# Graph attention over edges: values gathered by indirect DMA, and leaky ReLU split in two parts

## The reference, cut to what matters

```
Xq = H @ W_lin.T ; Xv = H @ W_val.T            # per node, split in 4 heads
e  = sum_d leaky_relu(Xq[src] + Xq[dst], 0.2) * a
e  = e + log(adj[src, dst] + 1e-8)
attn = softmax of e over the edges with the same src
Y[src] = sum over edges of attn * Xv[dst]
x  = layernorm(x + Y @ W_out.T)
```

## Time and profile before

| | us |
|---|---|
| median of 3 runs | 875.0 |
| all runs | 874.92, 875.27, 875.0 |
| span of the profiled execution | 876.8 |

### The profile page before, as it was taken

The page is one execution under the profiler, slowest core; times in us unless marked ns, Lnnn a source line. Parts: engine busy times, 40 slices in busy tenths (PEclk is TensorE's granted clock), DMA queues, the critical chain, the costliest instruction groups (busy, mean ns, idle before and its releaser), DMA issues.

```text
span 876.8 us, 15203 instructions
## 1 busy us (share of the span) xinstructions
PE 856.3 (98%) x5228; PEld 744.9 (85%) x5228; DVE 698.4 (80%) x1572; ACT 607.1 (69%) x1117; POOL 237.5 (27%) x562
## 2 busy tenths in 40 slices
PE   8999999999999999999999999999999999999996
PEld 7888888878778789999998887878887999999885
DVE  5888888868888878777777777767987787897986
ACT  3778878886766766767676666666896677776454
POOL 0233333340000000000000001003474355666766
PEclk9999999999999999999999999999999999999999
DMA  4222221000000001000000086777155010111223
GB/s 139 74 61 61 61 61 49 1 1 1 1 1 0 1 1 49 1 1 1 1 2 0 12 180 145 163 167 154 45 125 117 14 37 26 37 38 37 59 64 84
DMA packets 30988, 45.43 MB, mean 52 GB/s; under 512 B 2593, under 2 KB 23745, under 8 KB 27841
## 3 DMA queue, kind: packets, MB, share of 16 engines
q1 hardware_dynamic: 27680, 27.34, 10.8%
q0 software_dynamic: 2304, 16.78, 9.4%
q10 hardware_dynamic: 928, 0.35, 0.2%
HBM read 19.29 MB, written 8.39 MB: 32 GB/s over the span
## 4 chain that ended last, share of the span: by engine, by line
PE 79%; DVE 13%; ACT 4%; issue 2%; DMA 1%; POOL 1%; DVEq 0%; POOLq 0%; ACTq 0%
PE psum L505 7%; PE psum L506 7%; PE psum L507 7%; PE psum L523 6%; PE psum L519 6%; PE psum L520 6%; PE psum L1344 5%; PE psum L1266 5%; PE psum L412 3%; PE psum L454 3%; PE psum L1357 3%; PE psum L388 2%; PE psum L389 2%; PE psum L387 2%; PE psum L1324 2%
## 5 line engine op out<-in xcount | busy, mean ns | idle before, releaser
L646 ACT ACTIVATE work<-psum,bias 128x512 f32<-128x512 f32 (+1 forms) x408 | 232.1, 622 | 27.4 <-PE psum L523 26.0
L505 PE MATMUL psum<-hT_hi,w_hi 128*128 128x512 f32 (+1 forms) x406 | 148.2, 365 | 3.3 <-ACT work L646 2.8
L506 PE MATMUL psum<-hT_lo,w_hi 128*128 128x512 f32 (+1 forms) x406 | 146.5, 361 | 0.0
L507 PE MATMUL psum<-hT_hi,w_lo 128*128 128x512 f32 (+1 forms) x406 | 146.4, 361 | 0.0
L627 ACT ACTIVATE work<-work 128x512 f32<-128x512 f32 (+1 forms) x112 | 63.8, 570 | 108.9 <-DVE work L967 71.9
L978 DVE TENSOR_TENSOR work<-work 128x512 f32<-128x512 f32 (+1 forms) x111 | 68.6, 618 | 54.0 <-ACT work L627 54.0
L519 PE MATMUL psum<-hs_hi,w_hi 128*128 128x512 f32 (+1 forms) x288 | 103.9, 361 | 1.1 <-DVE hs_hi L912 0.9
L523 PE MATMUL psum<-hs_lo,w_hi 128*128 128x512 f32 (+1 forms) x288 | 104.5, 363 | 0.0
L520 PE MATMUL psum<-hs_hi,w_lo 128*128 128x512 f32 (+1 forms) x288 | 103.2, 358 | 0.0
L1172 POOL DMA_DIRECT2D hT_lo<-hT_hi x8 | 7.5, 937 | 351.3 <-DVE hT_lo L914 330.8
L505 PEld LDWEIGHTS psum<-hT_hi,w_hi 128*128 128x128 f32 x406 | 76.4, 188 | 17.4 <-ACT work L646 5.2
(11 more groups left out here) (225 smaller groups left out, 1902.9 us busy)
## 6 DMA issues: line engine op xcount, KB each, us to landing
work<-x_by_batch SPq DMA_DIRECT2D x32, 256.0 KB, 2.7
x_stage<-x_by_state SPq DMA_DIRECT2D x8, 1024.0 KB, 5.6
hT_lo<-hT_hi POOLq DMA_DIRECT2D x8, 1024.0 KB, 9.8
hT_lo<-x_stage POOLq DMA_DIRECT2D x8, 1024.0 KB, 7.2
out<-x_kept SPq DMA_DIRECT2D x31, 256.0 KB, 2.3
work<-L_gnn_Wih SPq DMA_DIRECT2D x4, 256.0 KB, 2.9
work<-L_gnn_Whh SPq DMA_DIRECT2D x3, 256.0 KB, 3.1
out<-x_kept SPq DMA_DIRECT2D x2, 128.0 KB, 2.3
```

The source lines that it names most:

```text
L505: pe.matmul(out, w_hi[:, w, g, :], xh, start=True, stop=False)
L506: pe.matmul(out, w_hi[:, w, g, :], xl, start=False, stop=False)
L507: mm = pe.matmul(out, w_lo[:, w, g, :], xh, start=False, stop=(t == 0))
L646: op = act.activation(gate[s][g][:, 0:ph.width], psum[:, 4 * s + g, 0:ph.width], ACT.Tanh if g == G else ACT.Sigmoid, bias=bias[:, b:b + 1])
```

## The change

The value product is no longer split. ACT copies it from the accumulator to the SBUF tensor `values`, SP stores it to a tensor in DRAM, and for every four tiles POOL issues two indirect DMAs (one for each half of the edges) that fetch for each edge the row of its `dst`. `value_gather` and `value_lo` are gone; `weight_values` multiplies in place.

Leaky ReLU becomes 0.8 relu(z) + 0.2 z. The linear part of the score is linear in the query, so the query weights get 4 more columns (0.2 W a, one for each head), and a query tile is 132 columns wide. Three batches fit in the accumulator bank, the fourth goes to another one. POOL copies the 4 columns of `xq_hi` and `xq_lo` to `linear` (`keep_linear`), where they stay until the group's scores are summed with two more products. As `xq_hi` and `xq_lo` have one buffer, the next `query_hi` waits for `linear_kept`.

```
     # POOL, run_gpsimd
+        def keep_linear(k):
+            g, n = divmod(k, GT)
+            pool.wait_ge(S["xq_ready"], 2 * k + 2)
+            if g >= 2:
+                pool.wait_ge(S["edges_psum"], g - 1)
+            for part, xq in enumerate((xq_hi, xq_lo)):
+                op = pool.tensor_copy(linear[:, g % 2, part, :, n, :], xq[:, :, P:QC])
+            op.then_inc(S["linear_kept"], 1)
+
+        def gather_values(j):
+            pool.wait_ge(v_stored[j % 2], 16 * GROUP * (j // 2 + 1))
+            pool.wait_ge(S["t_psum"], GROUP * (j + 1))
+            if j >= 2:
+                pool.wait_ge(S["va_ready"], EC * GROUP * (j - 2) + 1)
+            for c in range(EC):
+                pool.indirect_dma_start(out=values[:, c, tiles_of(j)], out_offset=None, in_=v_rows[j],
+                                        in_offset=bass.IndirectOffsetOnAxis(ap=dst_i[:, c:c + 1], axis=0)).then_inc(v_gathered[j % 2], 16)
         for n in range(LAST):
             if has(n - 3 - LAG) and not late(n - 3 - LAG):
                 normalize_out(n, n - 3 - LAG)
             if has(n + 2) or 0 <= n - 2 - LAG < last:
                 factors(n)
             ...
+            if has(n):
+                keep_linear(n)
+            j, part = divmod(n - GATHER_AFTER, GROUP)
+            if part == GROUP - 1 and 0 <= j < sums:
+                gather_values(j)
     # ACT
         def query_hi(k):
             act.wait_ge(S["factors_done"], k + 1)
-            act.wait_ge(S["q_psum"], k + 1)
-            for b in range(BT):
-                op = act.activation(xq_hi[:, b, :], psum[:, Q, b * P:(b + 1) * P], ACT.Copy, scale=scale_of(k, b))
-            op.then_inc(S["q_hi"], 1)
+            act.wait_ge(S["linear_kept"], k)
+            act.wait_ge(S["q_psum"], 2 * k + 1)
+            for b in range(IN_BANK):
+                act.activation(xq_hi[:, b, :], query_at(k, b), ACT.Copy, scale=scale_of(k, b))
+        def last_query_hi(k):
+            act.wait_ge(S["q_psum"], 2 * k + 2)
+            act.activation(xq_hi[:, IN_BANK, :], query_at(k, IN_BANK), ACT.Copy, scale=scale_of(k, IN_BANK)).then_inc(S["q_hi"], 1)
     # ACT, slot(n)
                 if not scaled_by_vector(n):
                     query_hi(n)
                 if n:
-                    value_hi(n)
+                    copy_value(n)
+                if not scaled_by_vector(n):
+                    last_query_hi(n)
     # DVE
         def query_hi(k):
             dve.wait_ge(S["factors_done"], k + 1)
-            dve.wait_ge(S["q_psum"], k + 1)
-            dve.tensor_tensor(xq_hi[:, :, :], by_bank(Q), ...)
+            dve.wait_ge(S["q_psum"], 2 * k + 2)
+            if k:
+                dve.wait_ge(S["linear_kept"], k)
+            dve.tensor_tensor(xq_hi[:, 0:IN_BANK, :], ...)
+            for b in range(IN_BANK, BT):
+                op = dve.tensor_scalar(xq_hi[:, b, :], query_at(k, b), scale_of(k, b), None, ALU.mult)
     # DVE, weight_values
+            va = values[:, c, tile_of(k)].rearrange("p (b h d) -> p b h d", b=BT, d=DH)
+            dve.tensor_tensor(va, va, w.unsqueeze(3).broadcast_to([P, BT, HEADS, DH]), ALU.mult).then_inc(S["va_ready"], 1)
     # PE, edge_scores, last tile of a group
+                pe.wait_ge(S["linear_kept"], k + 1)
+                for part in range(2):
+                    mm = pe.matmul(scores_of(g), linear[:, g % 2, part].rearrange("p b k h -> p (b k h)"), ends[:, :],
+                                   start=False, stop=(part == 1), skip_group_check=True)
     # SP
+        def store_values(k):
+            j, part = divmod(k, GROUP)
+            if j >= 2 and not part:
+                sp.wait_ge(v_gathered[j % 2], 16 * EC * (j // 2))
+            sp.wait_ge(S["v_copied"], k + 1)
+            sp.dma_start(v_rows[j][:, part * TW:(part + 1) * TW], values[:, 0, tile_of(k)]).then_inc(v_stored[j % 2], 16)
```

More of the change, by code:

```diff
@@ L1092, in odd, with tile_of, tiles_of, va_of @@
         return late(m) and m % 2 == 1
-    def gather_bank(m, c):
-        return (VG, T)[c] if not late(m) else (Z if odd(m) else Q) + c
     def sum_bank(m):
-        return T if odd(m) or m == first_late - 1 else YO
+        return T if odd(m) else YO
     def out_bank(m):
[L1102 to L1109, removed]
+        return YO if not late(m) else SCORE if odd(m) else Z + 1
+    def tile_of(k):
+        return slice(k * TW, (k + 1) * TW)
+    def tiles_of(j):
+        return slice(j * GROUP * TW, (j + 1) * GROUP * TW)
+    def va_of(k, c, b):
+        return values[:, c, k * TW + b * P:k * TW + (b + 1) * P]
     def mixing(n):
@@ L1149, in run_sync, with load_x @@
         region_free(sp)
-        for j in range(tiles // GROUP):
+        sums = tiles // GROUP
+        def load_x(j):
             if j:
@@ L1377, in slot @@
         def slot(n):
-            if n > 0 and n % GT == LAG % GT and has(n - LAG):
+            new_group = n > 0 and n % GT == LAG % GT and has(n - LAG)
+            if new_group and not has(n):
                 attention_by_edge((n - LAG) // GT)
@@ L1385, in slot @@
                 values(n)
+                if behind_values(n):
+                    last_query(n)
+            if new_group and has(n):
+                attention_by_edge((n - LAG) // GT)
             if n - 1 - LAG == last:
@@ L1488, in leaky_relu @@
             act.wait_ge(S["z_psum"], 2 * k + h + 1)
[L1489 removed]
+            act.activation(leaky[:, h], psum[:, Z + h, :].rearrange("p (b e) -> p b e", b=2), ACT.Relu, scale=1.0 - SLOPE).then_inc(
+                S["leaky_ready"], 1)
         def slot(n):
@@ L1661, in slot @@
         def slot(n):
-            new_group = n > 0 and n % GT == LAG % GT
-            if ahead(n - LAG) and not new_group:
+            new_group = n > 0 and n % GT == LAG % GT and has(n - LAG)
+            alone = has(n - LAG) and not has(n)
+            if alone and not new_group:
                 weight_values(n - LAG, 0)
@@ L1669, in slot @@
                 add_mixed(n - 2 - LAG)
-            if n > 0 and n % GT == LAG % GT and has(n - LAG):
+            if alone and new_group:
                 attention_out((n - LAG) // GT)
-            if ahead(n - LAG) and new_group:
                 weight_values(n - LAG, 0)
@@ L1678, in slot @@
                 stats_out(n, n - 2 - LAG)
-            if has(n):
-                if n:
-                    scaled_query(n)
-                value_lo(n)
+            if n and has(n):
+                scaled_query(n)
+            if new_group and not alone:
+                attention_out((n - LAG) // GT)
             g, part = softmax_at(n)
@@ L1685, in slot @@
                 softmax(g, step)
-            if has(n - LAG) and not ahead(n - LAG):
+            if has(n - LAG) and not alone:
                 weight_values(n - LAG, 0)
```

227 lines of the change are left out of this document (117 added, 110 removed).

## The result

The changed kernel takes 988.5 us (median of 4 runs, 984.96 to 991.45) against 875.1 (4 runs): 1.128 times as long, interval 1.125 to 1.131. The forecast was 988. A run's time is some 1.8 us above its own span: the profiled execution of the changed kernel took 987.7 us with a span of 985.9, so the one of before, with its span of 876.8, will have taken some 878.6, 3.5 more than the median. The trace is therefore compared span with span: +109.1.

The account below looks back on a forecast made before the run. PE (98% busy) was taken as the bound, DVE setting the early pace. Span 876.8 + 32.5 early + 82 middle - 2 late = 989.3, less 1.8 for the median: 987.5, say 988; range 950 to 1015.

Parts of the forecast that it names:

- The order: On POOL, keep_linear(n - 1) runs behind factors(n - 1), which waits for slot n's statistics: copies five microseconds late for the query.
- The ring: Middle slot: statistics, POOL's chain, query, product, add_mixed and next statistics wait in a circle; 11.0 us at full clock, 12.8 forecast.
- The clock: Middle stage: PE, waiting over 4 us a slot, runs most of gather and output at half speed; slot 12.8 for 11.0.
- The middle term of 82: Slots 15 to 30, all sixteen at 12.8 us for 7.67: 16 x (12.8 - 7.67) = +82.
- Rival A: Middle stage: the clock stays up, slots take 11.0 us, +53 for sixteen; 958 us in all; chance 15%.
- The early stage: Early slots take 6.0 us for 4.05, plus softmax steps, DMA issues and 1.5 for slots 12 to 14: +32.5.
- The late stage: Over 12 late slots, removed value products that partly filled PE's wait for copy_yT save 0 to 0.4 each: -2 us.
- The indirect DMAs: Issue on POOL taken as 0.94 us each, covered by POOL's wait for the next statistics: no loss.
- rival C: Indirect DMAs hold POOL for 9.8 us each, +104, so 1092 us; chance 5% in its full form.
- nothing but the gathers, six slots ahead of their use, waits for them: SP's stores of the values, queued ahead of output stores and behind the last load of x, delay nothing else.
- Rival B: The wait is harmless: PE saves 1.04 us in 19 middle slots, early 5, late 2; 848 us; chance 7%.
- The last term of the sum: The runs' median was taken to lie 1.8 us below the profiled span: 989.3 becomes 987.5.

Follow-up runs that it names:

- the wait alone: Kernel before plus only POOL copies of 4 columns to scratch behind factors(n), with query_hi waiting for them; values still by one-hot products: 977.1 us.
- one call moved: Changed kernel with keep_linear(n) run ahead of factors(n) on POOL for n >= 1: 881.9 us.
- PE kept busy: Changed kernel with 15 unused products of 128 columns on PE ahead of gather in each middle slot: 971.9 us.
- the fastest version: Changed kernel with copies ahead of factors and normalize_out, indirect DMA pairs issued in two slots, last accumulating load of x four slots later: 863.2 us.
- the way over DRAM alone: Changed kernel without keep_linear, its wait and the products with `linear`; stores and indirect DMAs stay: 867.1 us.
- more copies: Changed kernel with four more POOL copies of 16 elements behind keep_linear's two, each waiting for the one before, the next query for the last: 1018.2 us.
- With the fill: Changed kernel with four unused products of 128 columns on PE in slots 34 to 41 of the late stage: 988.3 us.
- the four kernels without the closed ring: Changed kernel with copies ahead of factors (881.9 us), that with normalize_out passed and gathers split (872.9), the fastest version (863.2), the way over DRAM alone (867.1).

## Why the prediction was right, and where it was not

**The order was read rightly.** That factors(n - 1) needs the statistics of slot n itself, so that a copy behind it can't be done when the query wants it, is what the slack in the earlier trace rows said; the wait alone makes 101 of 113 us, one call moved takes 107 away.

**The ring, step by step**, from the end of stats_in in the slot above (812.12): shift done at 4.00 (forecast 4.00), copies at 4.27 (4.5), the last xq_hi at 6.0 (6.3), query_lo at 7.2 (7.5), then gather and output at the lower clock to 10.5. Then come add_mixed, a wait of 0.36 for ACT's copy of the turned state, which the forecast did not have, and stats_in: 12.88. With PE kept busy output ends at 8.9 (forecast 9.0), and the slot is 812.73 - 801.85 = 10.88 (forecast 11.0 at full clock). The two copies took 0.33 in place of 0.5.

**The clock: right for a slot, wrong in how many slots have it.** The middle term of 82 measured 75.4. By window from add_mixed to add_mixed, the first slot, one of the three at 0.91 or 0.92, and the slot above:

```profile
713.04:722.62 9.58, 6.79 (x62) 6.18 (x61) 5.08 (x18) 4.85 (x10) 4.54 (x11) 1.00 0.27 84
835.21:846.97 11.76, 7.67 (x62) 7.07 (x62) 6.00 (x20) 5.67 (x12) 4.59 (x14) 0.91 0.14 47
809.77:822.65 12.88, 8.96 (x62) 8.36 (x61) 5.11 (x19) 5.69 (x12) 6.63 (x16) 0.76 0.38 124
```

Twelve of the sixteen slots, at 0.76 to 0.79, last 12.77 on average: the forecast's 12.8. Three at 0.91 or 0.92 last 11.63 to 11.84, which makes about 3.2 of the missing 6.6. Another 3.2 lie in the first slot, of 9.58: there factors still has the entering tile alone (its `rstd` takes 1.04 us for 1.67, and there is no shift), so the ring is shorter, and the clock stayed at 1.00. The sum took all sixteen as alike. With PE kept busy the slot is 11.30 on average, 1.08 less, a low estimate of what the clock costs, as the fill costs something too; between the two slots shown the difference is 12.88 - 10.88 = 2.0. Rival A, with no loss of clock, would have been 958; the run with PE kept busy, 971.9, lies 14 above it: its middle slots are 11.30 and not 11.0, and its late stage lasts 76.9 us.

The Trainium skill ("TensorE: Matmul & The Clock Gate", section "Loop structure matters more than you think") has it that a long wait for a DMA before every product costs PE its clock. Here the wait is for DVE, and the traces agree on the whole: 0.76 to 0.92 in fifteen slots, nearly all with waits of 2.6 to 4.1 us ahead of gather, and 1.00 in fifteen of sixteen where the fill cut these waits to at most 1.14. The length of the wait does not sort the slots: 4.09 us stand in one at 0.77 and in one at 0.91.

**The early stage**, 5.93 a slot for 6.0 and 6.86 with a DMA issue for 6.94, came to +30.3 for 32.5.

**The late stage was wrong in sign**: +3.4 for -2. The step that failed is "these products partly fill PE's wait for copy_yT: between 0 and 0.4 a slot". They filled it in full: without them PE waits 0.69 us for copy_yT in each plain late slot, and the slot lasts 3.63 as before, so their removal gave nothing:

```profile
963.04 1.16 PE L1409 MATMUL psum<-w_outT,yT 128*128 128x128 f32 x8 [0.69 <-ACT yT L1537]
```

And behind PE's wait for the last softmax the clock was low for longer than before. By window, the changed kernel, then the kernel before:

```profile
942.00:945.00 3.00, 3.00 (x16) 3.00 (x16) 2.64 (x9) 1.65 (x4) 2.53 (x10) 0.50 1.02 406
945.00:948.00 3.00, 2.31 (x11) 2.02 (x11) 1.33 (x3) 2.13 (x5) 2.53 (x11) 0.50 0.28 86
948.00:951.00 3.00, 3.00 (x17) 3.00 (x17) 2.34 (x9) 0.00 (x0) 0.80 (x4) 0.54 0.29 87
```

```profile
833.00:836.00 3.00, 1.50 (x13) 1.50 (x14) 2.93 (x10) 1.38 (x4) 2.42 (x9) 1.00 0.27 77
836.00:839.00 3.00, 3.00 (x14) 2.81 (x13) 2.27 (x8) 0.92 (x3) 0.96 (x6) 0.52 0.09 24
839.00:842.00 3.00, 3.00 (x25) 2.82 (x25) 2.65 (x8) 1.21 (x4) 2.16 (x7) 0.91 0.28 80
```

Some 9 us at about half clock in place of some 3. A sum_by_source of 1.95 us takes 3.76 there, and two slots are 2.7 us longer together. The missing products alone do not bring this about: three other kernels without them have a late stage of 71.0 (the fastest version), 71.2 (the way over DRAM alone) and 71.8 (more copies), with a slot of the last softmax of 6.3 to 7.0. With the fill only the second of the two slots came back. What does it stays open.

**The indirect DMAs**: 1.02 us of issue and some 0.3 before it, near the 0.94 taken; rival C falls. What the prediction did not see is the traffic of the way over DRAM beside the last load of x (no run separates the indirect DMAs from the stores). In the changed kernel the ring is so slow that POOL waits for none of it; as soon as the ring opens, that load and the accumulating DMA beside it are late where POOL needs them. The sentence "nothing but the gathers, six slots ahead of their use, waits for them" is right of the stores and overlooks who shares the DMA engines.

**Rival B**, a harmless wait, was priced at 848. With the wait opened in earnest the kernel stands at 863.2: the middle gains 0.90 a slot (16 slots), not 1.04 in 19, and neither the early nor the late stage gains anything.

That the total came out within 1 us is partly luck. In the trace -2.2, -6.6 and +5.4 in the three stages leave 3.4: the forecast added 112.5 to the span, and 109.1 were measured. But the medians lie 113.4 apart, as the profiled execution of before was some 3.5 above its median and that of the changed kernel 0.8 below. The last term of the sum, -1.8, set the span of one execution against the median of others: a run takes 1.8 us more than its own span, and the term came out right because the execution of before was 3.5 slow (876.8 + 1.8 - 3.5 = 875.1).

## What to carry to other kernels

Before adding a wait, look for what stands ahead of its releaser on the releaser's engine, and when that can start: two copies, 0.33 us together, cost 100 us because they were queued behind a chain that waits for the waiter. Engine shares say nothing here (POOL was 26% busy); the time between the consumer's start and the producer's start in the kernel before shows it. And where a ring leaves PE idle, price its products at both clock levels.

## What the hardware showed that was not expected

An f32 product of 128 columns ran as two instructions, 0.112 us each at full clock: 15 of them are 30 records and 3.62 us in the trace. A copy of 16 elements on POOL took 0.19 us, but is shown at some 0.5 right behind the issue of a DMA on that engine. The indirect DMAs of the changed kernel land in 6.2 to 12.7 us (median 7.9). In the four kernels without the closed ring the last load of x, which runs beside them, took 11.5 to 12.2 us (6.9 in the kernel before, 7.9 in the changed one), and the accumulating DMA from `hT_hi` beside it 13.3 to 14.6 (11.2 and 7.9).
